# Attention set-up: head 0 and its values start on the first row group; other rows are loaded later; three blocks of moments move into heads 2 to 4

## What is computed

```
x = x + L0_attn(layernorm(x)); x = x + L0_ffn(layernorm(x))
x = x + L1_attn(layernorm(x)); x = x + L1_ffn(layernorm(x))

L1_attn:  q, k, v = projections of layernorm(x), 16 heads of 64
          att = q k^T * scale, causal mask, softmax (minus the row maximum)
          z = W (softmax(att) v)
layernorm: (x - mean) / sqrt(var + 1e-5), over 256 columns
```

## Time and profile before

| | us |
|---|---|
| median of 3 runs | 2265.49 |
| lowest, highest | 2263.61, 2271.2 |
| the profiled execution, its own time | 2245.85 |
| its span, first to last instruction | 2243.9 |
| set-up of the attention: barrier to T(0) | 586 to 636 |
| T(0) to T(1) | 636.16 to 666.26 |
| T(1) to T(2) | 666.26 to 683.68 |

### The profile page before, as it was taken

How to read it: one execution, slowest core, us unless ns; L and a number is a source line. 1 busy time by engine, 2 the same in 40 slices (tenths; PEclk the granted TensorE clock), 3 DMA queues, 4 the chain that set the end, 5 groups by cost and what they waited for, 6 DMA issues and landing times. The chain is left out here.

```text
span 2243.9 us, 43076 instructions
## 1 busy us (share of the span) xinstructions
PE 1952.1 (87%) x11825; PEld 1458.9 (65%) x11826; DVE 1393.3 (62%) x3691; ACT 1058.3 (47%) x2206; POOL 1187.4 (53%) x1162
## 2 busy tenths in 40 slices
PE   4964999999579999899999899999899999956760
PEld 2553888888456676677777577777677777645650
DVE  6784434444566767657777656877656777647651
ACT  5331333333335555445555445555445555513760
POOL 3464332233226656435677626577635677826782
PEclk8767999999789999999999999999899999977885
DMA  9662333333402222112221111121101121123988
GB/s 335 216 207 79 51 51 52 50 51 50 130 17 55 54 55 53 41 27 56 64 62 49 35 31 51 49 54 42 46 23 51 49 55 47 40 94 117 204 134 250
DMA packets 206939, 178.07 MB, mean 79 GB/s; under 512 B 85563, under 2 KB 188824, under 8 KB 206113
## 3 DMA queue, kind: packets, MB, share of 16 engines
q1 hardware_dynamic: 176224, 143.37, 21.9%
q0 software_dynamic: 28800, 27.74, 8.2%
q10 hardware_dynamic: 1728, 4.73, 0.5%
HBM read 95.45 MB, written 80.86 MB: 79 GB/s over the span
## 5 line engine op out<-in xcount | busy, mean ns | idle before, releaser
L923 POOL TENSOR_TENSOR c_den<-c_den,c_p 128x512 f32<-128x512 f32 (+3 forms) x576 | 552.5, 959 | 372.1 <-ACT c_p L1198 301.1
L1198 ACT ACTIVATE c_p<-PS 128x512 f32<-128x512 f32 (+3 forms) x768 | 350.2, 487 | 350.7 <-PE PS L2379 238.8
L2400 PE MATMUL PS<-c_p,c_vh 128*64 128x256 f32 (+1 forms) x2816 | 336.1, 352 | 0.0
L2348 PE MATMUL PS<-c_k,c_q 128*128 128x512 f32 (+2 forms) x768 | 291.1, 380 | 29.8 <-DVE c_max L1740 21.5
L2371 PE MATMUL PS<-c_q,c_k 128*128 128x512 f32 (+2 forms) x768 | 293.8, 386 | 3.0 <-issue 1.5
L2400 PEld LDWEIGHTS PS<-c_p,c_vh 128*64 128x64 f32 x2816 | 198.4, 137 | 106.3 <-issue 52.8
L2372 PE MATMUL PS<-c_q,c_k 128*128 128x512 f32 (+2 forms) x768 | 259.8, 349 | 0.0
L861 POOL DMA_INDIRECT acc<-b_y,b_tok x72 | 112.1, 1557 | 273.4 <-ACT b_y L1104 251.4
L1189 ACT ACTIVATE c_q<-PS 64x512 fp32r<-64x512 f32 x256 | 151.2, 591 | 176.9 <-PE PS L2335 173.8
L1747 DVE CUSTOM_DVE_ANT_0 PS<-PS,c_maskq 128x128 f32<-128x128 f32 (+3 forms) x256 | 127.0, 500 | 144.7 <-PE PS L2348 138.4
L2348 PEld LDWEIGHTS PS<-c_k,c_q 128*128 128x128 f32 x768 | 147.3, 192 | 97.9 <-DVE c_max L1740 30.6
(11 more groups left out here) (294 smaller groups left out, 3962.8 us busy)
## 6 DMA issues: line engine op xcount, KB each, us to landing
c_vh<-c_v SPq DMA_DIRECT2D x64, 256.0 KB
c_rrow<-rden SPq DMA_DIRECT2D x64, 256.0 KB, 3.6
b_xt<-routed SPq DMA_DIRECT2D x72, 130.0 KB, 2.1
routed<-b_empty SPq DMA_DIRECT2D x32, 289.0 KB, 9.3
d_xe<-routed SPq DMA_DIRECT2D x32, 289.0 KB, 4.2
b_w12T<-in_w12T_dram SPq DMA_DIRECT2D x16, 512.0 KB, 12.7
acc<-X SPq DMA_DIRECT2D x16, 512.0 KB, 6.8
X<-acc SPq DMA_DIRECT2D x16, 512.0 KB, 7.4
```

The costliest lines, as they stand in the source:

```text
L923: pool.tensor_tensor(c_den[c][:, off:], c_den[c][:, off:], p, ALU.add).then_inc(s_cPa, 1)
L1198: act.activation(c_p[:, P_AT[m]:P_AT[m] + WIDTH[m]], PS[:, ST_BANK[m % ROUND], skip:skip + WIDTH[m]], ACT.Exp, scale=ATT_SCALE).then_inc(s ...
L2348: pe.matmul(PS[:, 2 + use[0], 0:max(w, 256)], c_q1[h][:, t * P:(t + 1) * P], c_k1[h][:, c * 512:c * 512 + max(w, 256)], start=True, stop=T ...
L2400: ins = pe.matmul(dst, c_vh[h][:, j, :], moving, start=(j == 0), stop=(t0 == 2 + a))
```

## The change

- **PE** transposes group 0, waits for both of its low parts (four lines of waits on `s_turn`), projects half 0 of head 0, makes value tiles 0 and 1, and only then transposes group 1. Tiles 2 and 3 follow, then half 1. In the loop over the 12 score chunks the tiles run two ahead of where they ran, so that tiles 4 to 12 stand ahead of chunks 0 to 8 and tile 13 ahead of chunk 10.
- **DVE** does the whole chain of group 0 (with both `low_qk`) before group 1. The low split of head 0's half 0 stands ahead of `c_xT_lo` of group 1. `low_qk(2, 0)` moves forward from behind M10, M11 to behind the split of head 1. Moments of groups 5, 6 and 7 leave the set-up for heads 2, 3 and 4 of the first batch, between chunks M8 and M9; the 24-wide `all_rstds` goes to the same place in head 5.
- **ACT** follows with its copies; `high_qk(2, 1, 0)` moves from behind value tiles 14 and 15 to ahead of tile 11.
- **SP** waits until `c_xT_hi` of group 0 is there (`s_cxh`) before it issues the loads of groups 2 to 7, and with them what is queued behind: two small weights and the stores of the split weights of heads 0 and 1.
- The normalised rows of the set-up get a buffer of their own, `first_xn`, as the value tiles now fill `c_v`, where `xn` lies, before group 1 has been transposed.

```diff
--- before.py
+++ after.py
@@ -253,6 +253,7 @@
         at[0] = v_at
         c_v = place("c_v", [P, QT, NH * DQ])
         c_vh = [place(f"c_vh_{h}", [P, QT, DQ]) for h in range(2)]
+        first_xn = nc.alloc_sbuf_tensor_at("first_xn", [P, G, D], F32, offset=at[0])
         c_p = place("c_p", [P, P_SIZE])
         c_den = [place(f"c_den_{c}", [P, 512]) for c in range(NC2)]
         c_max = place("c_max", [P, QT])
@@ -733,6 +734,7 @@
             for h in range(2):
                 stage_weights(h, h, False)
             stage_wo(0, 0)
+            sp.wait_ge(s_cxh, KD)
             for g in range(QT // G, NG):
                 load_x(g)
             sp.dma_start(r_swb[:, :], swT).then_inc(s_dl, 16)
@@ -1272,8 +1274,6 @@
                     for a in range(2):
                         take_v(b + 1, a, tables[NH])
 
-            for g in range(S // GT):
-                take_xT(0, g, first_turns())
             def first_hi(H, c):
                 for part in range(3):
                     split_hi(H, H, c, part)
@@ -1288,17 +1288,20 @@
                         act.wait_ge(s_cvt, n + 1)
                         act.sem_inc(s_cve, 1)
 
+            take_xT(0, 0, first_turns())
             first_hi(0, 0)
             take_first_v(0, 1)
+            take_xT(0, 1, first_turns())
+            take_first_v(2, 3)
             first_hi(0, 1)
-            take_first_v(2, 3, 4)
+            take_first_v(4, 5, 6)
             first_hi(1, 0)
-            take_first_v(5, 6, 7, 8)
+            take_first_v(7, 8, 9, 10)
             first_hi(1, 1)
-            take_first_v(9, 10, 11, 12, 13)
+            high_qk(2, 1, 0)
+            take_first_v(11, 12, 13)
             take_max(0, first_turns())
             take_first_v(14, 15)
-            high_qk(2, 1, 0)
             for m in range(ROUND):
                 probabilities(0, m)
             batch_exps(0, False, True)
@@ -1692,13 +1695,18 @@
                     st.done(dve.bn_stats(stat[:, q, :], tile_of(g * G, q)))
                 collect_moments(dve, st, g * G, G, stat, mv)
 
+            def load_moments(g):
+
+                dve.wait_ge(s_x[g], 32)
+                moments(g)
+
             def batch_moments(b):
 
                 for g in range(QT // G):
                     moments(b * (QT // G) + g)
                 all_rstds(dve, st, b * QT, QT)
 
-            def make_xn(batch, g):
+            def make_xn(batch, g, xn=xn):
 
                 if g:
 
@@ -1907,6 +1915,10 @@
                     add_z(b, pair - 1, (2, 3), table)
                 maxima(8)
                 routing(1)
+                if splits(b) and 5 <= hd + 3 < NG:
+                    load_moments(hd + 3)
+                if splits(b) and hd + 3 == NG:
+                    all_rstds(dve, st, QT, NT - QT)
                 if fetch:
                     make_xn(b + 1, 1)
                     maxima(9, 10, 11)
@@ -1951,20 +1963,26 @@
                 batch_moments(b)
 
             st.done(dve.memset(r_sum[:, :], 0.0))
-            def load_moments(g):
-
-                dve.wait_ge(s_x[g], 32)
-                moments(g)
-
-            for g in range(S // GT):
+            def first_rows(g):
                 load_moments(g)
                 all_rstds(dve, st, g * G, G)
-                if g:
-                    low_xT(0, g - 1, first_turns())
-                make_xn(0, g)
+                make_xn(0, g, first_xn)
+
+            def first_lo(H, c):
+                for k in range(2):
+                    split_lo(H, H, c, k)
+
+            def first_max(*chunks):
+                for n in chunks:
+                    maximum(0, n, first_turns(), "M")
+
+            first_rows(0)
             for h in range(2):
                 low_qk(h, h)
-            low_xT(0, S // GT - 1, first_turns())
+            low_xT(0, 0, first_turns())
+            first_rows(1)
+            first_lo(0, 0)
+            low_xT(0, 1, first_turns())
 
             dve.wait_ge(s_cset, 2)
             for m in (c_maskq, c_maskk):
@@ -1973,36 +1991,20 @@
                 st.done(dve.memset(c_k2[h][DQ:DQ + 1, :].bitcast(F32), 1.0))
             st.sync()
             dve.sem_inc(s_cset, 1)
-            table = first_turns()
-
-            def first_lo(H, c):
-                for k in range(2):
-                    split_lo(H, H, c, k)
-
-            def first_max(*chunks):
-                for n in chunks:
-                    maximum(0, n, table, "M")
-
-            first_lo(0, 0)
+            first_lo(0, 1)
             load_moments(2)
-            first_lo(0, 1)
             first_max(0, 1)
             first_lo(1, 0)
             first_max(2, 3)
             load_moments(3)
             first_max(4, 5)
             first_lo(1, 1)
+            low_qk(2, 0)
             first_max(6, 7)
             load_moments(4)
-            first_max(8, 9)
-            load_moments(5)
-            first_max(10, 11)
-            low_qk(2, 0)
-            load_moments(6)
+            first_max(*range(8, len(CHUNKS)))
             for n in range(4):
-                maximum(1, n, table, "N")
-            load_moments(7)
-            all_rstds(dve, st, QT, NT - QT)
+                maximum(1, n, first_turns(), "N")
             batch_steps(0, False, True)
             with dve.Fori(0, B - 2) as i:
                 st.loop(i, B - 2, BATCH_STEPS)
@@ -2295,7 +2297,7 @@
                 pe.sem_inc(s_turn[r], 1)
             parts = ((0, 0), (1, 0), (0, 1))
 
-            def transpose_x(batch, g, table):
+            def transpose_x(batch, g, table, xn=xn):
 
                 pe.wait_ge(s_cxn, batch * QT + (g + 1) * G)
                 for k in range(KD):
@@ -2581,9 +2583,6 @@
                     values(b + 1, 1, table)
 
             table = first_turns()
-            for g in range(S // GT):
-                transpose_x(0, g, table)
-
             def first_projections(H, c):
                 for step in range(3 * c, 3 * c + 3):
                     project(H, 0, H, step)
@@ -2600,13 +2599,23 @@
                         pe.wait_ge(s_cvt, n - 1)
                     value_tile(FIRST_V_BANK + n % 2, n // QT, n % QT)
 
+            transpose_x(0, 0, table, first_xn)
+            for k in range(KD):
+                r, turn = table[f"X{k}"]
+                pe.wait_ge(s_turn[r], turn + 1)
             first_projections(0, 0)
             first_values(0, 1)
+            transpose_x(0, 1, table, first_xn)
+            first_values(2, 3)
+            for k in range(KD, 2 * KD):
+                r, turn = table[f"X{k}"]
+                pe.wait_ge(s_turn[r], turn + 1)
             first_projections(0, 1)
 
             pe.wait_ge(s_cset, 3)
             for n in range(len(CHUNKS)):
-                first_values(n + 2)
+                if n <= 8 or n == 10:
+                    first_values(n + 4 if n <= 8 else 13)
                 if n == 2:
                     first_projections(1, 0)
                 if n == 6:
```

## The result

| | before | changed kernel |
|---|---|---|
| median of 12 runs, us | 2265.81 | 2256.03 |
| lowest, highest | 2258.91, 2280.49 | 2247.26, 2263.07 |
| profiled execution, own time and span | 2245.85, 2243.9 | 2260.97, 2258.3 |

The ratio is 0.9942, with a 95% interval from 0.9923 to 0.9961. The kernel is faster by 0.58%, some 13 us (9 to 17 by the interval), and even the weak end of the interval is beyond 0.3%. The two medians of the table lie 9.8 us apart (0.43%), which is inside that interval.

What follows compares the result with a forecast made beforehand. PE was taken to bound steady heads, while set-up PE waited on DVE's chain. Terms -1.8 - 11.7 + 2.6 = -10.9 us gave 2254.6 us from a 2265.49 median; range 2247 to 2263.

Steps and rivals of the forecast that it cites:

- head 5: Square roots moved behind M8: 2.4 us on DVE, 1.6 fitting its gap, so 0.8 us comes back.
- T(0) to T(1): Set-up's end and head 0: two PE waits go, clock partly recovers; 30.1 becomes 18.4 us, 11.7 shorter.
- The start of the set-up: First weight split waits out POOL; PE starts 4.6 us earlier, group 1's low parts end 2.4 us later.
- From there to T(0): DVE from group 1's low parts to M11: 27.2 us instead of 31.2, making T(0) 1.8 us earlier.
- Heads 2 to 4: A moments block between M8 and M9 delays each head by 0.6 us, 1.8 us over three heads.
- (a): Rival: inserts in heads 2 to 5 cost their full 12.6 us, giving 2264.6 us, no change; 10%.
- the prediction's own signs: Right: T(3) to T(6) each 0.6 to 0.9 us later; wrong: steps of heads 2 to 5 longer by 2 or more.
- (b): Rival: PE's waits for N0 and M6 move and stay, leaving -2.7 us, 2262.8 us; 8%.
- (c): Rival: PE cannot start before 603 in the set-up, losing the 4.6 us, 2259.2 us; 6%.
- (d): Rival: broken-up start keeps PE's clock at half in the set-up, +14 us, 2279.6 us; 4%.
- Moved and costed at nothing: Later loads of x on SP, ACT's moved copies and split, and PE's extra waits on low parts add nothing.

Runs made afterwards that it cites:

- e8: The changed kernel run again with no edit: 2271.37 us, ratio 0.9951 to the kernel before.
- the mended ones: Four kernels where POOL waits for the weight splits, roots spread over heads 5 to 8, moments blocks cut in two: ratios 0.9895 to 0.9903 to before.
- e1: Kernel before with the weight split, moments and roots moved, without the early start of head 0: 2233.94 us beside 2249.22.
- e5: Kernel before with only the moments of groups 5 to 7 and the square roots moved: 2261.21 us beside 2281.86.
- e4: Changed kernel with the twelve square-root operations spread over heads 5 to 8, three each: 2233.20 us beside 2249.22 of the kernel before.
- e2: Kernel before with only the weight split for head 2 moved earlier on ACT and DVE: 2244.93 us beside 2249.22.
- e10: Mended kernel without the early start of head 0, both masks scaled ahead of the weight splits: 2258.62 us, ratio 0.9899 to the kernel before.
- e6: Changed kernel with the six loads of x issued at once, without SP's wait: 2268.89 us beside 2280.98 of the kernel before.
- e12: Second execution of the changed kernel with the six loads of x issued at once: 2237.83 us beside 2245.53 of the kernel before.

## Why the prediction was right, point by point

**The time.** The forecast of -10.9 us stands beside -8.5 in the trace (at T(9)), -9.8 between the medians and -13 by the ratio (interval -9 to -17). The gain was named in the right place. That the sum came so close is in part luck: it holds an error of 2.9 us (head 5) and one of 1.8 us the other way (T(0) to T(1)). The marks come from one profile of each kernel, and e8 gives -9.4 at T(9) against the same profile of before. The times show more than the marks in the other kernels too: in the mended ones the medians differ by 21 to 24 us and T(9) by 16 to 18. Why is not settled. A part may be that the one profile of the kernel before caught POOL late (3.41 us of normalising), while e1 and e5, with the same start of the set-up, took 5.5 and began their first projection 1.8 us later.

**The start of the set-up: right in one of its two cases.** The step said that up to the normalised group 0 nothing changes and the first weight split waits out POOL. In the changed kernel's profile it was the other way round: normalising lasted until POOL was done, both splits took 0.75, and PE started at 13.52 instead of 12.4. In e8, the same code, it went as forecast: the splits took 2.90, PE started at 12.18, and T(0) came at 48.21 for 48.4. What the step missed is that there are two cases. The 3.41 us of group 0 in the earlier trace rows were taken as fixed, although the next paragraph put them down to POOL. In the first case group 1's low parts were done at 22.3 against 21.1 forecast, late by 1.2 as PE's start was by 1.1.

**From there to T(0): right.** Forecast 27.2 us to the end of M11; measured 26.6 (618.97 to 645.6). DVE's waits for ACT's high parts were 1.31, 1.60 and 2.21 us, 5.1 together, for 4.7 forecast. The 1.0 us that M10 and M11 were to wait for PE did not come: DVE's longest wait from M8 to M11 was 0.23. These two make up the difference of 0.6. T(0) came 1.0 us earlier, for 1.8.

**T(0) to T(1): right in mechanism, 1.8 us too cautious.** The 4.27 and 3.9 us are gone. T(0) to the first product of head 0 proper took 6.83 us (7.5 forecast), and head 0 9.73, for the 10.93 of head 1 that the step had taken as its measure.

**Heads 2 to 4: right.** Each was to come 0.6 us later; measured 0.66, 0.67 and 0.69, with M9 at 694.48 behind the block and PE waiting 0.39 for it. Rival (a), the full 12.6 us, is refuted: T(1) to T(9) grew by 6.1.

**Head 5: the term that was mis-sized.** The roots were put at 2.4 us, of which 0.8 would show: it was 3.65. The first step of the error is "POOL rests in this place". POOL had rested for 4.63 us, but its denominators began at 755.07, within the roots, which took 3.6 us (752.99 to 756.6) and not 2.4; one of the twelve operations, with its 1.24 us, makes up 1.1 of the difference. The second is that a wait of 1.94 us on PE also cost the clock, and with it the other 1.7 us. e4 took both away and gave 3.65 back. This term alone is 2.9 us too small, more than the whole 2.4 between forecast and T(9); of the rest, T(0) was 0.8 worse, T(0) to T(1) 1.8 better, and the other heads together 0.6 worse. By the prediction's own signs this place was wrong: it had named steps of heads 2 to 5 longer by 2 us or more as a sign against it, and T(6) 0.6 to 0.9 us late as one for it.

**Rivals.** (b), that the two waits stay, is refuted by the rows of waits; it would have been right for the weight split alone (e2, 5.98 us). (c), that PE starts no earlier, is false as said, since PE did start 3.5 us earlier. But its core holds: DVE sets T(0), and the early start is worth little, 1.9 us at T(0) and 0.5 at T(9) beside e1, 0.9 at T(0) and nothing at T(1) beside e10. (d), a clock that stays low, did not come; it came in small, 1.2 to 1.5 us in a fall at T(0).

**Moved and costed at nothing.** Right for the loads (e6, e12). One small thing is open: the step over head 1 is 17.58 to 17.62 us in every kernel that moves the moments, though none of them stand in that head, and 17.42 before and 17.44 in e2.

## What to carry to other kernels

Starting the bottleneck engine earlier is worth only what the engine that feeds it can follow with; look at which chain sets the end of the stretch, and move work out of that chain (here the moments and roots out of DVE's set-up) before reordering the other engine. Work that is moved into a gap is cut to the gap: three short operations in each of four heads cost next to nothing, twelve in one cost 3.65 us. And a duration in the profile that is known to be disturbed by another engine is not a constant: ask for the quiet one, and who would be disturbed instead. One profile shows one of the cases; a second one of the same code (e8) showed the other.

## What the runs showed of the hardware

- **DVE against POOL, whole operations at a time.** Normalising four tiles of 128x256 took 1.38 us alone and 3.4 or 5.5 us beside POOL's 128x1024 subtractions of 2.35 us each. Less than a tenth of a us in POOL's start decides between the two. Where it was 3.5 (e8), the weight splits behind it took 2.90 us together instead of 0.75. Scaling a 128x512 mask took 0.29 or 2.32, a 128x24 step of the roots 0.18 or 1.24.
- **TensorE's granted clock fell in short stretches within busy work.** It went from 1.00 to 0.50 for 3 to 4 us after a single wait of 1.94 us (head 5) and, in six executions of seven, after waits of 0.8, 0.2, 0.9, 0.4 and 1.2 us spread over the last 7 us ahead of T(0). The same code, with the same waits, did it in one execution and not in another (e12, e6), on two chips. That the waits are the cause is not shown.
- **The loads of x** took a median of 7.3 to 7.8 us to land whether issued at once or 12.7 us into the attention, and nothing waited for them.
